# Keys, values, queries and latent values of a decoder layer as split operands in three passes, with normed rows parked in device memory

## What is computed

```
nq  = rms(x @ w_cq);   q = [nq @ dq_nope, rope(nq @ dq_rope)]        # 16 heads, 32 + 64
ckv = rms(x @ w_ckv);  k1 = [ckv @ dk_nope, rope(x @ w_krope) / 16];  v1 = ckv @ w_dv
sel = x[top 64 tokens by x @ w_imp]                                  # per batch row
ks, vs = sel @ w_selk (with rope), sel @ w_selv
kw, vw = x @ w_wink (with rope), x @ w_winv
out = g0*attn(q,k1,v1,causal) + g1*attn(q,ks,vs) + g2*attn(q,kw,vw,causal);  x = ln(x + out @ w_proj)
x = ln(x + cross_attention(x, ctx))
x = ln(x + sum over e of route[e] * (relu(x @ W1[e] + b1[e]) @ W2[e] + b2[e]))
```

## Time and profile before

| | us |
|---|---|
| median of 3 runs | 1701.59 (1699.93 to 1704.69) |
| the profiled execution | 1698.96 |
| its span, first to last instruction | 1697.2 |
| mean granted clock of TensorE | 0.99 |
| TensorE busy | 1633.6 |
| GpSimd busy | 1040.7 |
| VectorE busy | 1166.4 |
| ScalarE busy | 835.6 |

### The profile page before, as it was taken

The page is one execution under the profiler, slowest core; times in us unless marked ns, Lnnn a source line. Parts: engine busy times, 40 slices in busy tenths (PEclk is TensorE's granted clock), DMA queues, the critical chain, the costliest instruction groups (busy, mean ns, idle before and its releaser), DMA issues.

```text
span 1697.2 us, 33804 instructions
## 1 busy us (share of the span) xinstructions
PE 1633.6 (96%) x11448; PEld 1342.9 (79%) x11448; DVE 1166.4 (69%) x3826; ACT 835.6 (49%) x2768; POOL 1040.7 (61%) x1461
## 2 busy tenths in 40 slices
PE   6899999999999999999998799999999999999998
PEld 5586786776777868767776489999999999999997
DVE  4568767877787678777775588567556665657557
ACT  1566947948758579488486632222222222222221
POOL 2566756847657567477475677566666565657553
PEclk9899999999999999999999899999999999999999
DMA  7203003012031030120211020001010101010001
GB/s 220 66 2 84 19 25 78 2 45 57 2 74 28 16 86 2 45 57 2 65 32 51 2 69 29 28 1 50 1 50 1 51 1 50 1 51 1 1 1 50
DMA packets 52460, 63.54 MB, mean 37 GB/s; under 512 B 12288, under 2 KB 40448, under 8 KB 52160
## 3 DMA queue, kind: packets, MB, share of 16 engines
q1 hardware_dynamic: 51568, 58.62, 12.5%
q10 hardware_dynamic: 720, 2.75, 0.5%
HBM read 29.89 MB, written 2.10 MB: 19 GB/s over the span
## 4 chain that ended last, share of the span: by engine, by line
PE 77%; POOL 6%; DVE 6%; ACT 6%; issue 5%; DMA 0%; DVEq 0%; POOLq 0%; ACTq 0%
PE ps_Y L2246 21%; PE ps_H L2246 20%; PE ps_S L1450 17%; PE ps_O L1450 5%; ACT pr L890 5%; PE ps_X L1450 5%; PE ps_T L1679 4%; POOL pr L726 3%; PE ps_T L1450 2%; PE ps_T L1799 1%; POOL rot L666 1%; PE ps_S L1799 1%; DVE sm L1361 1%; POOL rot L676 1%; DVE h_hi L2209 1%
## 5 line engine op out<-in xcount | busy, mean ns | idle before, releaser
L2034 POOL TENSOR_TENSOR h_lo<-h_sb,h_hi 128x512 fp32r<-128x512 f32 x256 | 363.5, 1448 | 107.1 <-DVE h_hi L2209 107.1
L2080 ACT ACTIVATE h_sb<-ps_H,b_sb 128x512 f32<-128x512 f32 x256 | 176.7, 690 | 503.7 <-PE ps_H L2246 475.5
L691 POOL TENSOR_TENSOR pr<-pr,rden 128x128 f32<-128x128 f32 (+2 forms) x768 | 307.2, 436 | 85.3 <-DVE rden L1242 84.9
L2209 DVE CAST h_hi<-h_sb 128x512 fp32r<-128x512 f32 x256 | 247.0, 985 | 122.4 <-ACT h_sb L2080 122.2
L890 ACT ACTIVATE pr<-sm,nmx 128x128 f32<-128x128 f32 (+2 forms) x768 | 311.8, 414 | 23.1 <-DVE nmx L1253 23.0
L2246 PE MATMUL ps_Y<-w_hi,h_lo 128*128 128x256 f32 x1024 | 286.5, 280 | 0.0
L2246 PE MATMUL ps_Y<-w_hi,h_hi 128*128 128x256 f32 x1024 | 286.5, 280 | 0.0
L2246 PE MATMUL ps_Y<-w_lo,h_hi 128*128 128x256 f32 x1024 | 286.4, 280 | 0.0
L726 POOL TENSOR_TENSOR pr<-pr,rden 128x256 f32<-128x256 f32 x256 | 150.6, 615 | 111.1 <-DVE rden L1242 110.8
L1253 DVE CUSTOM_DVE_ANT_0 sm<-ps_S,cmask 128x128 f32<-128x128 f32 (+2 forms) x768 | 192.6, 308 | 33.9 <-PE ps_S L1450 25.0
L2246 PE MATMUL ps_H<-x_hi,w_hi 128*128 128x512 f32 x512 | 199.8, 390 | 0.0
(11 more groups left out here) (265 smaller groups left out, 3121.2 us busy)
## 6 DMA issues: line engine op xcount, KB each, us to landing
qT_sb<-rot SPq DMA_DIRECT2D x256, 64.0 KB, 2.0
w_raw<-in_W SPq DMA_DIRECT2D x16, 1024.0 KB, 6.2
kT_sb<-rot SPq DMA_DIRECT2D x192, 64.0 KB, 2.0
xin<-in_x SPq DMA_DIRECT2D x8, 256.0 KB, 2.8
cin<-in_ctx SPq DMA_DIRECT2D x8, 256.0 KB, 2.7
w_kw<-in_wink ACTq DMA_DIRECT2D x2, 768.0 KB, 5.8
w_ks<-in_selk SPq DMA_DIRECT2D x2, 768.0 KB, 5.5
out<-x SPq DMA_DIRECT2D x3, 512.0 KB, 3.1
```

The costliest lines, as they stand in the source:

```text
L691: last = pool.tensor_tensor(p_, p_, rden[:, h % 2, n:n + 1].to_broadcast([P, width]), ALU.mult)
L2034: pool.tensor_tensor(h_lo[:, s % 2, ht, :], h_sb[:, ht % 4, :], h_hi[:, s % 2, ht, :].bitcast(F32), ALU.subtract).then_inc(lo_sb.sem, 1)
L2080: ins = act.activation(h_sb[:, ht % 4, :], pst[plan.bank(f)][:, :], ACT.Relu, bias=b1[:, 2 * i + s // NCH, ht:ht + 1])
L2209: dve.tensor_copy(h_hi[:, s % 2, ht, :], h_sb[:, ht % 4, :]).then_inc(hi_sb.sem, 1)
```

## The change

The weights and activations of the keys, window values and queries products are split into high and low halves, and each product becomes three passes per pair of operands. ScalarE makes the high halves and VectorE the low ones of the weights, once, during front 0. The high half of `xT` is made by ScalarE and the low half by GpSimd in each front; those of the query latents by VectorE (`latq_hi`, `latq_lo`). For the latent values, whose contraction has only 32 rows, the four strips of 32 partitions hold high and low halves of latents (`lat4`: high, high, low, low from the top strip down) and of weights (`w_dv4`, high and low by turns), so that one pass over 128 rows sums all four terms. The latent keys and the selected keys and values keep full precision.

SBUF has no room for all of this at once. The weights `w_ks` of the selected keys and the low halves of `w_kw` share one place: both are reloaded in every front, the second from a copy in device memory (`kept_lows`, 1.5 MB). The normed rows of batch rows 0 to 6 are written to device memory (`kept_rows`, 256 KB each) and read back before the expert stage; their old place is used by `tie`, `xT` and others. `cmp1` and `cmp2`, in which `own_scores` and `beaten_by` write, lie over the two halves of `xT`; so these wait for the last window values product, and they are put one step later.

```diff
-        self.w_qd = put("w_qd", 0, [P, 4, HW])
-        self.w_kw = put("w_kw", 8192, [P, NC, 3, HW])
-        self.w_ks = put("w_ks", 20480, [P, NC, 3, HW])
-        self.w_vw = put("w_vw", 32768, [P, NC, HW])
-        self.w_vs = put("w_vs", 36864, [P, NC, HW])
+        self.w_q = tuple(put(n, at, [P, 4, HW], F32R) for n, at in (("w_q_hi", 0), ("w_q_lo", 8192)))
+        self.w_vw = tuple(put(n, at, [P, NC, HW], F32R) for n, at in (("w_vw_hi", 16384), ("w_vw_lo", 20480)))
+        self.w_kw = tuple(put(n, at, [P, NC, 3, HW], F32R) for n, at in (("w_kw_hi", 24576), ("w_kw_lo", 104448)))
+        self.w_dv4 = put("w_dv4", 36864, [P, HW], F32R)
+        self.latq_lo = put("latq_lo", 38912, [P, T], F32R)
+        self.lat4 = put("lat4", 39936, [P, T], F32R)
+        self.w_ks = put("w_ks", 104448, [P, NC, 3, HW])
+        self.w_vs = put("w_vs", 116736, [P, NC, HW])
+        self.raw_kw = put("raw_kw", 57344, [P, NC, 3, HW])
+        self.raw_vw = put("raw_vw", 69632, [P, NC, HW])
...
+        self.tie = put("tie", 120832, [P, NT, T])
+        self.cmp1 = put("cmp1", 122880, [P, NT, T])
+        self.cmp2 = put("cmp2", 124928, [P, NT, T])
+        self.xT_hi = put("xT_hi", 122880, [P, NC, T], F32R)
+        self.xT_lo = put("xT_lo", 124928, [P, NC, T], F32R)
+        self.rt3 = put("rt3", 126976, [P, HW])
...
-            load(w_ks[:, 0, :, :], w["selk"][0:P], w_late_in)
-            load(w_ks[:, 1, :, :], w["selk"][P:C], w_late_in)
...
+            def selected_weights(i):
+
+                sp.wait_ge(plan.full_sem(("kw", 1, "n")), plan.after(("kw", 1, "n"), i))
+                if i == 0:
+                    sp.wait_ge(s_kept, 16)
+                sp.dma_start(w_ks[:, 0, :, :], w["selk"][0:P]).then_inc(ks_in.sem, 16)
+                sp.dma_start(w_ks[:, 1, :, :], w["selk"][P:C]).then_inc(ks_in.sem, 16)
+
+            def key_lows(i):
+
+                sp.wait_ge(plan.full_sem(("ks", "nv")), plan.after(("ks", "nv"), i))
+                sp.dma_start(w_kw[1][:, :, :, :].rearrange("p c s n -> p (c s n)").bitcast(F32), kept_lows[:, :]
+                             ).then_inc(kw_back.sem, 16)
+
+            def keep_rows(i):
+
+                sp.wait_ge(x2_sb.sem, x2_sb.at(i, 1))
+                sp.dma_start(kept_rows[i], x1[:, :, :].rearrange("p t c -> p (t c)")).then_inc(x2_kept.sem, 16)
+
+            def rows_again(a, b):
+
+                sp.wait_ge(x2_kept.sem, x2_kept.at(b, 0))
+                sp.dma_start(sh.x2[:, NT * a:NT * b, :].rearrange("p (i t) c -> p i (t c)", t=NT),
+                             kept_rows[a:b].rearrange("i p n -> p i n")).then_inc(x2_back, 16)
...
+                    if u == 1:
+                        selected_weights(i)
...
+                if i + 1 < NB - 1:
+                    key_lows(i + 1)
+                else:
+                    sp.wait_ge(rope_out.sem, rope_out.at(i + 1, 11))
+                    for g in range(2):
+                        sp.wait_ge(plan.free_sem(("ksT", g)), plan.after(("ksT", g), i + 1))
+                    rows_again(0, i)
+                keep_rows(i)
...
+            sp.wait_ge(w_low, 6)
+            sp.dma_start(kept_lows[:, :], w_kw[1][:, :, :, :].rearrange("p c s n -> p (c s n)").bitcast(F32)
+                         ).then_inc(s_kept, 16)
...
-                for _ in range(3):
-                    yield
+                yield
+                pool.wait_ge(x_high.sem, x_high.at(i, 1))
+                pool.tensor_tensor(xT_lo[:, :, :], xT[:, :, :], xT_hi[:, :, :].bitcast(F32), ALU.subtract
+                                   ).then_inc(x_low.sem, 1)
+                yield
...
+            act.wait_ge(w_keys_in, 16 * N_KEYS)
+            for s in (1, 2, 0):
+                for c in range(NC):
+                    act.copy(w_kw[0][:, c, s, :], sh.raw_kw[:, c, s, :]).then_inc(w_high, 1)
+
+            def other_weights_high():
+
+                act.wait_ge(w_mid_in, 16 * N_MID)
+                for c in range(NC):
+                    act.copy(w_vw[0][:, c, :], sh.raw_vw[:, c, :]).then_inc(w_high, 1)
+                for s in (1, 2, 0):
+                    act.copy(w_q[0][0:QL, s, :], raw_q[:, s, :]).then_inc(w_high, 1)
+                act.copy(w_dv4[:, :], raw_dv).then_inc(w_high, 1)
 
...
+                act.wait_ge(xT_done.sem, xT_done.at(i, 1))
+                act.copy(xT_hi[:, :, :], xT[:, :, :]).then_inc(x_high.sem, 1)
...
+                act.wait_ge(plan.free_sem("latT"), plan.after("latT", i))
+                for j in (3, 2):
+                    act.copy(lat4[HD * j:HD * j + HD, :], latT[QK:P, :]).then_inc(lat4_high.sem, 1)
...
+            def key_weights_low():
+                for n, (s, c) in enumerate((s, c) for s in (1, 2, 0) for c in range(NC)):
+                    dve.wait_ge(w_high, n + 1)
+                    dve.tensor_tensor(w_kw[1][:, c, s, :], sh.raw_kw[:, c, s, :], w_kw[0][:, c, s, :].bitcast(F32),
+                                      ALU.subtract).then_inc(w_low, 1)
+
+            def other_weights_low():
+                for c in range(NC):
+                    dve.wait_ge(w_high, 6 + c + 1)
+                    dve.tensor_tensor(w_vw[1][:, c, :], sh.raw_vw[:, c, :], w_vw[0][:, c, :].bitcast(F32),
+                                      ALU.subtract).then_inc(w_low, 1)
+                for n, s in enumerate((1, 2, 0)):
+                    dve.wait_ge(w_high, 8 + n + 1)
+                    dve.tensor_tensor(w_q[1][0:QL, s, :], raw_q[:, s, :], w_q[0][0:QL, s, :].bitcast(F32),
+                                      ALU.subtract).then_inc(w_low, 1)
+                dve.wait_ge(w_high, 12)
+                for j in (0, 2):
+                    part = w_dv4[HD * j:HD * j + HD, :]
+                    dve.tensor_tensor(part, raw_dv[HD * j:HD * j + HD, :], part.bitcast(F32), ALU.subtract
+                                      ).then_inc(w_low, 1)
+                dve.wait_ge(s_absorbed, 1)
+                dve.tensor_tensor(w_q[1][0:QL, 3, :], pst["S0"][0:QL, :], w_q[0][0:QL, 3, :].bitcast(F32),
+                                  ALU.subtract).then_inc(w_low, 1)
...
-                dve.tensor_copy(latT[0:QL, 0, :], ps("latT")[0:QL, 0:T])
-                dve.tensor_copy(latT[:, 1, :], ps("latT")[:, T:2 * T]).then_inc(plan.free_sem("latT"), 1)
+                dve.tensor_copy(latq_hi[0:QL, :], ps("latT")[0:QL, 0:T]).then_inc(c.step(), 1)
+                dve.tensor_copy(latT[:, :], ps("latT")[:, T:2 * T])
+                dve.wait_ge(c.sem, c.value())
+                dve.tensor_tensor(latq_lo[0:QL, :], ps("latT")[0:QL, 0:T], latq_hi[0:QL, :].bitcast(F32), ALU.subtract
+                                  ).then_inc(plan.free_sem("latT"), 1)
+                yield
+
+                dve.wait_ge(plan.full_sem(("vw", 1)), plan.after(("vw", 1), i))
                 own_scores()
-                yield
...
+                dve.wait_ge(lat4_high.sem, lat4_high.at(i, 2))
+                for j in (1, 0):
+                    dve.tensor_tensor(lat4[HD * j:HD * j + HD, :], latT[QK:P, :], lat4[QK:P, :].bitcast(F32),
+                                      ALU.subtract).then_inc(lat4_low.sem, 1)
...
+                if f == "proj" and not first_row(i):
+                    dve.wait_ge(x2_kept.sem, x2_kept.at(i, 0))
...
-                    dst = x1[:, t, :] if k == 1 else sh.x2[:, NT * i + t, :]
+                    dst = sh.x2[:, NT * i + t, :] if k == 2 and i == NB - 1 else x1[:, t, :]
...
-                        for c, (w_, x_) in enumerate(zip(weights, moving)):
-                            last = mm(ps(name)[:, T * b:T * b + T], w_[:, block_], x_, c == 0, c == len(weights) - 1)
+                        terms = [x for hi, lo in zip(zip(weights[0], moving[0]), zip(weights[1], moving[1]))
+                                 for x in split_terms(hi, lo)]
+                        for n, (w_, x_) in enumerate(terms):
+                            last = mm(ps(name)[:, T * b:T * b + T], w_[:, block_], x_, n == 0, n == len(terms) - 1)
...
                 def keys(t, s):
-                    turned_product(("kw", t, "nab"[s]), [w_kw[:, c, s, :] for c in range(NC)],
-                                   [xT[:, c, :] for c in range(NC)])
+                    turned_product(("kw", t, "nab"[s]), [[k[:, c, s, :] for c in range(NC)] for k in w_kw],
+                                   [[x[:, c, :] for c in range(NC)] for x in (xT_hi, xT_lo)])
 
                 def window_values(t):
-                    product(i, ("vw", t), P, HW, tok(xT, t), [w_vw[:, c, :] for c in range(NC)])
+                    terms = [x for c in range(NC) for x in split_terms(
+                        (tok(xT_hi, t)[c], w_vw[0][:, c, :]), (tok(xT_lo, t)[c], w_vw[1][:, c, :]))]
+                    product(i, ("vw", t), P, HW, *zip(*terms))
 
                 def queries(t, s):
-                    turned_product(("q", t, "nabc"[s]), [w_q[:, s, :]], [latT[0:QL, 0, :]])
+                    turned_product(("q", t, "nabc"[s]), [[k[0:QL, s, :]] for k in w_q],
```

(12 more changed lines are left out.)

101 lines of the change are left out of this document (66 added, 35 removed).

## The result

The changed kernel takes 1709.8 us in the median of 9 runs (1706.17 to 1722.69), the kernel before 1702.48 of 9 (1699.71 to 1709.02): ratio 1.0046, 95% interval 1.0026 to 1.0066. It is slower by about 8 us. Ratios leave out an execution that is over 1.5% above the fastest of its kernel, which is here one of e9_mended, at 1725.7 us. The profiled execution took 1708.83 us, its span is 1707.1; the span before was 1697.2, so the two traces differ by 9.9 us. The prediction's range held the time, but its likeliest case, 1697 to 1707 us, did not come.

A forecast was written before the change was run, and what follows sets the result against it. TensorE is busiest, but VectorE's nearly full stretches were taken to absorb most of its savings. From 1698.96 us, +3 at the start and -2 over seven rows gave 1700; the median's 2.6 us offset made it 1702, range 1684 to 1711.

The forecast's parts named there:

- its likeliest case: Whole kernel: no change that a measurement can tell, 1697 to 1707 us, chance 0.43.
- A row: Steady attention row: about 0.2 to 0.3 us shorter, -2 us over seven rows.
- before the projection: Two keys products: TensorE waits about 0.5 us for xT's low half, gets back 2 x 0.32; net -0.1 us.
- projection to the first scaling: Four keys products: TensorE's saved 1.3 us becomes waiting for VectorE, except a gain of 0.16 us.
- the copies to the rotation: First cross heads, VectorE from the latT copies: the added latq_lo subtraction costs +0.34 us.
- the second latent values: Late in a row, beside cross scores: the product now runs alone, 0.23 us for no cover; nothing either way.
- The queue: DMA transfers: reloads and row writes all hidden in a steady row; at the start two w_ks issues add 0.9 us.
- The start: Before the first row: splitting delays the rotation 2.2 us, w_ks issues add 0.9; +3 us, bounds 0 and +6.
- ScalarE's first high half ends near 23.4: Front 0: eight VectorE splitting operations of 0.65 us follow this copy, so rotation products start 3.6 us later, at 28.6.
- Last row and experts: Row 7 and expert stage: added waits are for transfers 20 us and more old, so 0.
- rival C: VectorE's full stretch, latT to rotation: added work costs 1 us a row, +3 at the start; 1711 us, chance 0.22.
- B: Steady rows: VectorE's full stretches have give, 1 to 3 us a row saved; 1681 to 1697 us, chance 0.27.

The follow-up runs named there:

- e9_mended: Changed kernel with w_lo1 64 bytes lower, front 0's weight high halves earlier, w_ks later, and xT_lo passes last in the first keys product; 1707.52 us, ratio 1.0016.
- e6: Changed kernel without VectorE's subtraction that makes latq_lo, queries products reading latq_hi instead; 1713.52 us in a single run.
- e8: Changed kernel with the second latent values product of a row reading one strip of 32 partitions instead of four; 1708.45 us in a single run.
- e7: Changed kernel without the reloads of w_ks and w_kw_lo after front 0; 1711.5 us in a single run.
- e10: Changed kernel with extra TensorE work: a fourth term in four queries products, first latent values product made three times; 1707.07 us, ratio 1.0014.
- e3: Changed kernel with front 0's two w_ks transfers issued behind the second unit's last four key moves instead of ahead; 1710.8 us, ratio 1.0052.
- e1: Changed kernel with w_lo1 moved 64 bytes lower, onto a multiple of 128 bytes; 1706.81 us, ratio 1.0025.
- e2: Kernel before the change with w_lo1 moved 64 bytes higher, off the multiple of 128 bytes; 1710.17 us, ratio 1.0040.
- e5: Changed kernel with one pass, high times high, in place of three for keys, window values and queries; 1732.91 us in one run.
- e11: e9_mended with the extra TensorE work of e10 added; 1696.25 us, ratio 0.9948.

## Why the prediction was right and wrong

- **A row** (-0.2 to -0.3 us predicted, -0.5 measured). The reading held: TensorE's busy time fell by 3.3 us (I had said 5), and the saving turned into waits at 612 to 617. By its pieces: before the projection -0.08 (predicted -0.1); projection to the first scaling -0.39 (-0.16); from there to the copies of latT -0.22 (nothing); the copies to the rotation +0.09 (+0.34, a mis-sized term: e6 gives 0.06, since VectorE had slack toward the scores of heads 2 and 3); two queries products -0.3 (-0.3); behind them +0.5 up to the scores at 55.55, of which the second latent values are 0.3 by e8 (nothing). That the row came out near the forecast is thus partly errors that cancel. A keys product took 1.62 us from start to start, not 1.41: its first pass stands 0.2 us ahead of the second, a cost that the price from long series in the expert stage didn't have.
- **The queue.** Hidden in a row, as predicted (e7). At the start "Two w_ks issues inside the chain add 0.9" was too small: from the first key move to the first row's end it is 82.07 us after and 80.1 before, 2 us more (2.2 to 2.4 in e10 and e7). The two issues took 1.05 (47.84 to 48.89), and 0.8 went when e3 took the wait for the moves behind them away; the rest is in small gaps of the queue that no run takes apart.
- **The start** (+3 predicted with bounds 0 and +6, +7.15 measured). The mechanism was right, the size wrong, in this execution outside the bounds. The step that failed there is that ScalarE's first high half ends near 23.4: it stands behind the wait for the absorbed product, which ended at 25.38, not 22.2. Of these 3.2 us, 1.1 are a first product that starts at 15.44 instead of 14.36 (15.03 or later in every split kernel), and 2.1 the small products that took 5.32 us instead of 3.25. Only the 1.1 belongs to the change. In e7, with short small products, the rotation starts at 28.48 and the key moves at 31.75, where I had said 28.6 and 31.8, and the start is 4.5 us longer than before: inside the bounds, and the term that is too small there is the queue. The first bound, 0 "(if the queue catches up)", could not happen: there is no gap in it.
- **Experts: 0 predicted, +4.67 measured.** The step that failed stands under "Last row and experts": "its added waits are for transfers 20 us and more old: 0". I priced the waits and not the addresses, though the change moves buffers of that stage. This is the largest error of the change itself, and e1 and e2 show it both ways.
- **The clock.** No step of mine spoke of it. I priced TensorE's new waits at nothing. In the trace of before the clock stays up through all seven rows, but that was one execution of a kernel whose time goes up and down with the clock; that more waits could bring it down was not weighed. The Trainium skill ("TensorE: Matmul & The Clock Gate", "HAM oscillation — how this bites in real kernels" and "A second HAM failure mode: psum-queue depth-cycling") describes kernels whose clock falls again and again when TensorE waits between groups of products. The first section's waits are for transfers and longer than any here (1.12 us at most in a row after the change); the second's are short idle times, and it is the one that resembles this case. Read so, it speaks for a cost in clock, and so for rival C; e5, and e11 against e9, agree, while the falls at 44 us in e10 and e11 don't fit a simple form of it.
- **The sum and the sign.** +7.15 - 3.06 + 1.14 + 4.67 = 9.9 us; about 1.8 of the first term (the later key moves of the long small products) and most of the third are low stretches of the clock in this one execution, which leaves 7, near the 8 of the ratio. The sum of the prediction, 1702, missed by 8 us; that the range held the time is its width, which rival C gave it. C, slower, came true by its number and not by its mechanism: VectorE's stretch from latT to the rotation didn't grow by 1 us, but by 0.09. (B's 1681 to 1697 is 1684 to 1698 by its own price of 1 to 3 us a row and +3 at the start.)

What stays open: why the 64 bytes matter; why the clock falls in one row and not in the next with the same waits, and which wait brings it down; which of the fillings gave e11 its 11 us, since they were not tried one by one; and whether the kernel before would gain from filling too (not tried).

## What to carry to other kernels

Price a change by the engine whose chain is continuous between two hand-overs, not by the busiest engine: 3.3 us less for TensorE gave 0.5. When a change moves buffers, compare their addresses, down to 64 bytes, in stages that it does not touch too. And when the busiest engine starts to wait in short pieces, look at its granted clock over several executions: work in these waits that the result doesn't need was worth 11 us in the mended kernel. Compare the starts of two profiles only after a series of products that both do alike; here one such series differed by 2.1 us from execution to execution and made an experiment look twice as good as it was.

## What the runs showed of the hardware

- TensorE with w_lo1 moved by 64 bytes (e2 against before, after against e1): 48 passes of 512 columns 11.09 instead of 10.91 us, 96 of 256 columns 11.38 instead of 11.27.
- Falls of the granted clock to 0.50 in the rows lasted 3.4, 6.8, 10.2, 13.6, 20.5 and 37.5 us.
- The record of the clock can miss a low stretch. In the changed kernel's profile the key passes from 25.86 to 28.00 stand 0.21 us apart with a granted clock of 1.00, and 0.12 apart from 28.57 on; in e3's they stand 0.21 apart in 26 to 28 us, where the window gives 0.54, and 0.12 after 27.82. So the 2.1 us of the small products ahead of these passes are most likely clock too: where they took 5.32 us (six profiles) no fall is on record before 32 us, and where they took 3.25 or less (eight) one of 3.4 us begins at 21.3 to 24.4. The same page of the Trainium skill warns, in "Seeing it yourself", that such events are not always reliable; the trace agrees.
